# Neighbouring matmuls of one shape, one scan of both heads, and tiles projected a slot ahead in a fused Mamba layer and FFN

## The reference, cut to what matters

```python
proj = einsum('bsd,de->bse', rmsnorm(x), in_proj_w)       # z, x|B|C, dt
xBC = silu(conv4(proj[x|B|C]) + conv_b)                   # 4 taps along the tokens
dA = exp(softplus(dt_raw + dt_bias) * -exp(A_log))
h = dA_t * h + (dt_t * x_t) * B_t                         # for each token, 64x64 per head
y = h . C_t + D * x
g = groupnorm(y * silu(z)) * gate_norm_w
out = residual + g @ out_proj_w
```

## Time and profile before

| what | value |
|---|---|
| median of 3 runs (lowest, highest) | 1144.11 us (1141.79, 1144.46) |
| profiled execution, its span | 1145.73 us, 1143.9 us |
| busy: PE, PEld, DVE | 1033.2 us (90%), 732.0 us (64%), 1059.9 us (93%) |
| busy: ACT, POOL | 970.0 us (85%), 868.6 us (76%) |
| mean granted PE clock | 0.959 |

### The profile page before, as it was taken

The page is one execution under the profiler, slowest core; times in us unless marked ns, Lnnn a source line. Parts: engine busy times, 40 slices in busy tenths (PEclk is TensorE's granted clock), DMA queues, the critical chain, the costliest instruction groups (busy, mean ns, idle before and its releaser), DMA issues.

```text
span 1143.9 us, 26227 instructions
## 1 busy us (share of the span) xinstructions
PE 1033.2 (90%) x8912; PEld 732.0 (64%) x8912; DVE 1059.9 (93%) x2004; ACT 970.0 (85%) x2836; POOL 868.6 (76%) x596
## 2 busy tenths in 40 slices
PE   1724789999999999999999999999999999996797
PEld 1603566676666666676666666766666666664576
DVE  7597999999999999999999999999999999989474
ACT  2767898999999999999999999999999999984464
POOL 7300356888888888888888888888888888885765
PEclk9955899999999999999999999999999999997899
DMA  6320000000000000000000000000000000021001
GB/s 170 117 86 0 10 1 2 1 1 2 1 30 2 2 2 29 2 2 2 29 2 2 2 29 2 2 2 29 2 1 1 21 1 2 1 78 46 1 29 46
DMA packets 28084, 22.58 MB, mean 20 GB/s; under 512 B 11696, under 2 KB 22576, under 8 KB 27824
## 3 DMA queue, kind: packets, MB, share of 16 engines
q1 hardware_dynamic: 25136, 20.90, 5.9%
q10 hardware_dynamic: 2816, 0.02, 0.1%
HBM read 12.78 MB, written 8.13 MB: 18 GB/s over the span
## 4 chain that ended last, share of the span: by engine, by line
PE 77%; DVE 14%; issue 3%; POOL 2%; ACT 2%; DMA 0%; POOLq 0%; DVEq 0%; ACTq 0%
PE bank L1713 10%; PE bank L1695 10%; PE bank L1625 8%; PE bank L1727 8%; PE bank L1641 8%; PE bank L1626 6%; PE bank L1627 6%; PE bank L1681 5%; PE bank L1662 5%; DVE conv L1191 4%; PE bank L1766 3%; PE bank L1738 2%; DVE lm L1181 2%; PE bank L1555 1%; PE bank L1746 1%
## 5 line engine op out<-in xcount | busy, mean ns | idle before, releaser
L1191 DVE SCALAR_TENSOR_TENSOR conv<-bank,cw,conv 128x509 f32<-128x509 f32 (+2 forms) x576 | 421.7, 743 | 16.6 <-ACT conv L762 8.6
L636 POOL TENSOR_TENSOR lm<-lm,cbs 128x1024 f32<-128x1024 f32 x128 | 304.3, 2377 | 75.7 <-ACT xw L866 75.7
L1181 DVE TENSOR_TENSOR_SCAN lm<-bank,ident 128x512 f32<-128x512 f32 x256 | 298.7, 1210 | 0.7 <-PE bank L1641 0.6
L911 ACT ACTIVATE xdt<-bank,dt_all 128x64 f32<-128x64 f32 x1024 | 222.3, 329 | 37.2 <-PE bank L1662 37.2
L866 ACT ACTIVATE xw<-xdt,lm 128x64 f32<-128x64 f32 x768 | 199.3, 365 | 0.0
L644 POOL TENSOR_TENSOR ssum<-ssum,sq 128x512 f32<-128x512 f32 x96 | 123.1, 1283 | 93.0 <-ACT sq L926 92.8
L1625 PE MATMUL bank<-xn_hi,w_hi 128*128 128x512 f32 x320 | 166.1, 519 | 13.8 <-DVE conv L1191 13.1
L615 POOL TENSOR_TENSOR gated<-gated,gate 128x512 f32<-128x512 f32 x128 | 164.9, 1288 | 15.9 <-DVE gated L1238 14.5
L626 POOL TENSOR_TENSOR gated<-gated,rbs 128x512 f32<-128x512 f32 x120 | 153.8, 1282 | 0.0
L877 ACT ACTIVATE conv<-bank,cb_bias,cw 128x512 f32<-128x512 f32 x189 | 142.6, 781 | 11.5 <-PE bank L1627 7.3
L1713 PEld LDWEIGHTS bank<-lm,xdt 128*64 128x64 f32 x2048 | 110.3, 137 | 63.7 <-issue 63.7
(11 more groups left out here) (217 smaller groups left out, 1766.5 us busy)
## 6 DMA issues: line engine op xcount, KB each, us to landing
lm<-in_L_attn_in_proj_w SPq DMA_DIRECT2D x1, 2048.0 KB, 11.7
xn_scratch<-chan SPq DMA_DIRECT2D x4, 512.0 KB, 4.6
r_stage<-residual_scratch SPq DMA_DIRECT2D x8, 256.0 KB, 2.9
xn_stage<-xn_scratch SPq DMA_DIRECT2D x7, 256.0 KB, 3.2
x_scratch<-r_stage SPq DMA_DIRECT2D x7, 256.0 KB, 2.0
gate<-in_L_attn_hidden_states SPq DMA_DIRECT2D x2, 512.0 KB, 4.6
cdec<-in_L_attn_hidden_states SPq DMA_DIRECT2D x2, 512.0 KB, 7.1
w_out<-in_L_attn_out_proj_w SPq DMA_DIRECT2D x8, 128.0 KB, 3.3
```

Of the source, the lines that this page charges most:

```text
L636: gp.tensor_tensor(lm[:, mr, :, :], lm[:, mr, :, :], cbs[:, :, :], ALU.mult).then_inc(m_done, 1)
L911: act.activation(xdt[:, r, at:at + HP], misc_of("xt", n)[:, at:at + HP], ACT.Copy, scale=dt_h).then_inc(xdt_done, 1)
L1181: V.tensor_tensor_scan(lm[:, m % R, a, :], bc_bank[(3 * m + a) % 2][:, :], ident4[:, :], 0.0, ALU.mult, ALU.add).then_inc(scanned, 1)
L1191: V.scalar_tensor_tensor(out=conv[:, ci % 4, shift:S], in0=tile_bank(b, n, t)[:, 0:S - shift], scalar=cw[:, q, t, KW - 1 - shift:KW - shif ...
```

## The change

1. **Side by side.** On PE, `states`, `y_within` and `y_states` of a slot follow each other (`inner`), and the spread rows of the running products and of the next pair's first head come ahead of them; the second head's row comes behind.
2. **One scan.** The two spread rows of the decays lie in two neighbouring banks (`decays`), and DVE scans both heads in one instruction of 1024 columns. The row of the second head now waits for `decay_c` of the pair before it, in the same bank.
3. **State steps.** The copy of the first chunk's state goes from DVE to ACT (`first_state`). The chunks' end products are taken once for all, by 16 small products and one copy in slot 4 of the first sequence; the copy in each slot (L1221) goes.
4. **Second slot a slot early.** Tiles 3 and 4 are projected at the end of the first slot (`next_tile`), around `cb_products`, and ACT begins them there (`next_convolve`); `weigh` of the second slot is also done there (`weigh(1)`). `variance` and its copy go to the end of the first slot.
5. **Order of the second slot.** `b_transposes` comes ahead of `out_product`, `factor_transposes` behind it, z last.
6. **Factors.** The root is taken in POOL's second slot, and POOL instead of ACT copies it to 512 columns (`rexp`).
7. **Out product.** Its operands change places: four products with 128x128 pieces of `gated` as weights and 128 columns of `w_out`, so rows come out token-major; ACT's copy and PE's four transposes at a sequence's end go, and DVE adds the residual from the bank a slot earlier (`output_rows`).

DVE's taps come before `decay_c`, and its state steps behind it, in all slots (not shown). Cut to its core:

```diff
+def early_tile(b, n, t):
+    return n % R == 1 and t in PLAN[1] and (b, n) != (0, 1)
...
             n = 4 * q + r
+            plan += [(n, "xt", LAG_SSD, 0), (n, "s", LAG_STATE, 0)]
             if r == 0:
-                plan.append((n, "var", LAG_VAR, 0))
-            if r < 2:
-                plan += [(n, "s", LAG_STATE, 0), (n, "xt", LAG_SSD, 0)]
-            else:
-                plan += [(n, "xt", LAG_SSD, 0), (n, "s", LAG_STATE, 0)]
-            if r == 0:
-                plan += [(n, "cb", LAG_SSD, 0), (n, "cb", LAG_SSD, 1)]
+                plan += [(n, "cb", LAG_SSD, 0), (n, "cb", LAG_SSD, 1), (n, "var", LAG_VAR, 0)]
             if r == 1:
-                plan.append((n, "bt", LAG_M, 0))
-                plan.append((n, "rbc", LAG_FACTOR, 0))
+                plan += [(n, "bt", LAG_M, 0), (n, "rbc", LAG_FACTOR, 0)]
             if n == XO_SLOT:
-                plan.append((n, "xo", SLOTS, 0))
+                plan.append((n, "unused", SLOTS, 0))
...
+                    after(gp, rstd_done, UNITS, bb, v)
+                    after(gp, rbc_ready, UNITS, bb, v - 1)
+                    gp.tensor_copy(rexp[:, :, :], rtok[:, :].unsqueeze(2).broadcast_to([P, 2 * CH, HP])).then_inc(rexp_done, 1)
...
                 gate_product()
                 if r == 0:
                     decay_product()
                     normalise()
+                elif r == 1:
+                    normalise()
                     root()
+                    decay_product()
+                    square_sum()
...
+                def first_state():
+                    if back(b, n, LAG_STATE) is None:
+                        return
+                    bb, m = back(b, n, LAG_STATE)
+                    after(act, s_ready, SLOTS, bb, m)
+                    after(act, y_ready, SLOTS, bb, m - 2)
+                    act.activation(hpk[:, m % 2, 0, :], misc_of("s", n)[:, 0:NS], ACT.Copy).then_inc(hfirst, 1)
+                def next_convolve(k):
+                    if real and early_tile(b, n + 1, PLAN[1][k]):
+                        begin(PLAN[1][k], n + 1)
...
                     weigh()
                     convolve()
                     activate(0)
+                    scale_x()
+                    first_state()
+                    square()
+                    gate_silu()
+                    weigh(1)
+                    next_convolve(0)
+                    copy_cb()
+                    next_convolve(1)
                     copy_variance()
+                elif r == 1:
+                    convolve()
+                    activate(0)
+                    first_state()
                     scale_x()
                     square()
+                    copy_bt()
+                    copy_factor()
                     gate_silu()
-                    copy_cb()
-                elif r == 1:
...
-                    for a in range(2):
-                        after(dve, bc_ready, 3 * SLOTS, bb, 3 * m + a)
-                        V.tensor_tensor_scan(lm[:, m % R, a, :], bc_bank[(3 * m + a) % 2][:, :], ident4[:, :], 0.0,
-                                             ALU.mult, ALU.add).then_inc(scanned, 1)
+                    after(dve, bc_ready, 3 * SLOTS, bb, 3 * m + 1)
+                    V.tensor_tensor_scan(lm[:, m % R, :, :].rearrange("p a s -> p (a s)"), decays[:, :], ident4[:, :], 0.0,
+                                         ALU.mult, ALU.add).then_inc(scanned, 1)
...
-                    if c == 0:
-                        after(dve, s_ready, SLOTS, bb, m)
-                        after(dve, y_ready, SLOTS, bb, m - 2)
-                        V.tensor_copy(hpk[:, m % 2, 0, :], sbank[:, 0:NS]).then_inc(hstep, 1)
+                    if c == 1:
+                        after(dve, hfirst, SLOTS, bb, m)
+                        if (bb, m) == (0, 0):
+                            dve.wait_ge(pend_done, 1)
                     else:
-                        after(dve, hstep, 3 * SLOTS, bb, 3 * m + c - 1)
-                        V.scalar_tensor_tensor(out=hpk[:, m % 2, c, :], in0=hpk[:, m % 2, c - 1, :],
-                                               scalar=pend[:, m % R, c:c + 1], in1=sbank[:, NS * c:NS * c + NS],
-                                               op0=ALU.mult, op1=ALU.add).then_inc(hstep, 1)
...
-                i = 3 * m + k
-                pm, pk = divmod(i - 2, 3)
-                if pk < 2:
-                    after(pe, scanned, 2 * SLOTS, bb, 2 * pm + pk)
+                if k == 1:
+                    after(pe, cdec_done, SLOTS, bb, m - 1)
                 else:
-                    after(pe, cdec_done, SLOTS, bb, pm)
+                    after(pe, scanned, SLOTS, bb, m - 1 if k == 0 else m)
                 if isinstance(bb, int) and (bb, m, k) == (0, 0, 0):
                     pe.wait_ge(pr_rest, len(PR_ORDER))
                 first = (0, P, HP)[k]
...
+                def next_tile(k):
+                    if real and early_tile(b, n + 1, PLAN[1][k]):
+                        project(b, n + 1, PLAN[1][k], (b, n + 1))
...
-                    last = MM(out_bank[:, :], w_out[:, m, :], gated[:, (m // R) % 2, m % R, :], start=(m == 0), stop=(m == SLOTS - 1))
+                        after(pe, x1_done, 1, bb, -1)
+                        if bb == 0:
+                            pe.wait_ge(pend_done, 1)
+                    for c in range(CH):
+                        tok = slice(P * c, P * c + P)
+                        last = MM(out_bank[:, tok], gated[:, (m // R) % 2, m % R, tok], w_out[:, m, :],
+                                  start=(m == 0 and c == 0), stop=(m == SLOTS - 1 and c == CH - 1))
...
+                def inner():
+                    states()
+                    y_within()
+                    y_states()
                 if r == 0:
                     out_product()
                     tiles()
-                    variance()
-                    states()
+                    transposes()
                     gate_tile()
-                    transposes()
-                    y_within()
                     rows(ssd, 2)
                     rows(ahead, 0)
-                    y_states()
+                    inner()
+                    rows(ahead, 1)
+                    next_tile(0)
                     cb_products()
+                    next_tile(1)
+                    variance()
                 elif r == 1:
                     tiles()
-                    states()
                     transposes()
-                    out_product()
-                    y_within()
                     rows(ssd, 2)
                     rows(ahead, 0)
-                    y_states()
+                    inner()
+                    rows(ahead, 1)
+                    b_transposes()
+                    out_product()
+                    factor_transposes()
                     gate_tile()
-                    b_transposes()
-                    factor_transposes()
                 elif r == 2:
                     tiles()
                     transposes()
-                    states()
+                    rows(ssd, 2)
+                    rows(ahead, 0)
+                    inner()
+                    rows(ahead, 1)
                     out_product()
-                    y_within()
+                    gate_tile()
+                else:
+                    tiles()
+                    transposes()
+                    out_product()
+                    gate_tile()
                     rows(ssd, 2)
-                    y_states()
-                    gate_tile()
                     rows(ahead, 0)
-                else:
-                    transposes()
-                    states()
-                    tiles()
-                    gate_tile()
-                    y_within()
-                    rows(ssd, 2)
-                    out_product()
-                    rows(ahead, 0)
-                    y_states()
+                    inner()
+                    rows(ahead, 1)
                     next_input()
-                    last_output()
-                rows(ahead, 1)
```

200 lines of the change are left out of this document (81 added, 119 removed).

## The result

The changed kernel takes **1179.3 us** (median of 4 runs, 1176.4 to 1180.1) against 1144.3 for the kernel before on the same chip: a ratio of **1.030 [1.027, 1.033]**, slower, and outside the range of 1121 to 1155.

The account below looks back on a forecast made before the run. PE bounded the kernel before; after the change, an ACT-PE loop of 28.48 us a unit. Steady part -3.8, start -1, tail +3 on 1145.7, then 1.6 off to the median: about 1142 us, range 1121 to 1155.

Parts of the forecast that it names:

- PE's work: PE's matmuls in a unit, four units a sequence: cheaper in the new order, 27.0 us needed instead of 28.6.
- DVE's work: DVE's steps in a unit: copies and one scan start leave each slot, about 1.0 us less, 27.3 of 28.3 remain.
- ACT: ACT's list in a unit: loses the root's copy, gains four state copies at 0.20 us each; about even.
- POOL's: POOL's added 512-column copy, one a unit: between nothing and 1.28 us, about 1.0 in the tail; room for it.
- The turn is 28.48 us, longer than any engine's work: Loop of ACT (12.76 + 8.14) and PE (7.58) through `cbs` and `variance`, setting the unit's time; chance 0.45.
- Variance: End of the first slot: PE waits some 1.5 us a unit at `variance` for ACT's copy of `cbs`.
- Start: Before the steady part: DVE saves, slot 4 gains products and a copy; -1 us, bounds -5 and +3.
- Tail: After the last sequences: POOL's root and copy come behind feed-forward additions, PE's factors wait; +3 us, bounds 0 and +7.
- PE does not wait at `variance`: Rival, end of the first slot: a loop through DVE's scans decides, 27.85 us a unit, 1125 us; chance 0.24.
- The state copies lengthen ACT's turn: Rival, ACT's list: state copies at up to 0.33 us each make a unit 28.87, about 1153 us; chance 0.21.
- Bare weight loads: Rival, out product on PE: exposed loads add 0.64 us a slot, 29.5 a unit, about 1168 us; chance 0.04.
- DVE as the bound: Rival: DVE set the pace all along, 27.3 us a unit, 110.4 a sequence, 1110 us; chance 0.06.

Follow-up runs that it names:

- the last version: Changed kernel with variance and next input earlier, three DVE edits, POOL's decay product first, root and out product earlier in the tail: 1140.7 us, 0.997 of the kernel before.

## Why the prediction was wrong, point by point

- **PE's work** (28.6 to 27.0): right in its terms, as far as rows show them (0.40, 0.98, 0.80, an out product 0.81 to 0.90). Busy time could not have shown it: 114.59 us of a sequence against 115.44 in the earlier trace rows; why it hardly fell is not shown. The Trainium skill (Perfetto Trace Analysis, Identifying the Most-Contended Engine) says that matmul busy time is no good measure of headroom; this trace agrees.
- **DVE's work** (28.3 to 27.3): mis-sized. Busy time, 112.28 a sequence less 1.2, in four, is 27.8. Steps from start to start, waits left out, show where it went: a sequence of DVE's list took 114.7 us and now takes 113.0. The copies, the scan and `decay_c` gave back 4.1, as priced (0.25 in each of 16 slots); but the state steps took 1.0 more and the taps 1.3 more. Taps, copies and `decay_c` had stood between steps that wait for each other, and in the first and the fourth slot some of these stand back to back now: two state steps take 0.51 (584.70 to 585.21), where each takes 0.18 beside a tap (577.48 to 577.66); the last section has the taps. In the last version the list takes 113.2 of a sequence's 114.2.
- **ACT** about even: right; a state copy steps 0.10 to 0.15 us, half of what I took. **POOL's** copy was 0.61 (I took about 1.0).
- **"The turn is 28.48 us, longer than any engine's work"**: this is the step that failed, in two ways. It summed ACT's list as if it ran almost without a gap: reckoned 20.90, measured 21.47 (573.15 to 594.62), with gaps of 0.16, 0.4 and POOL's 0.12 in it; PE's part is 7.85 instead of 7.58. And it looked for a loop of two engines, where the round goes through four. What was not priced is what part 5 ties together: `out_product` stands behind the rows, the groups and B, with DVE's `skip` of the same slot waiting on it, and the text never follows who waits for `out_step`. That ties DVE to the end of PE's second slot, PE's second slot to ACT's copy, that copy to POOL's leg and the fourth slot, and the fourth slot to DVE again. The product's place alone is not the cost: put back ahead of the rows it changed nothing, since the row and the states behind it tie the same slot to DVE and ACT, and the fastest version keeps part 5's order in the steady part. What cost time is the length of that round, 29.33 us where DVE's own work is 27.8: 0.9 us less in PE's second slot made a plain unit 0.9 shorter, 0.44 more in ACT's fourth slot made it 0.46 longer. A unit takes 29.5, over the 28.9 that I had named as my bound.
- **Variance**: PE waits there for `cbs`, as said; it is 0.4 us instead of 1.5, and taking the variance off that place gave 14 us. So the place was right and the loop around it was not.
- **Start** (-1, bounds -5 and +3): +2.0 to the first mark, within the bounds.
- **Tail** (+3, bounds 0 and +7): +13.4. The mechanism (root behind the feed-forward step) is right and its size wrong: it held up the second-last unit too, and in the traces 4 to 8 us hang on it. The out product behind the rows, which I had not looked at there either, holds some 2 more; the rest stays open.
- **Rivals**: "PE does not wait at `variance`" did not come true; it waits, and no unit got shorter. "The state copies lengthen ACT's turn" had the direction and named the fourth slot, where ACT "gets there with almost nothing in hand", but not the cause: the copies cost half of what I took, and 0.44 us more in the third slot cost nothing. Bare weight loads: no, 0.81 to 0.90. DVE as the bound: not in the changed kernel, where it waits for 5 us of a sequence; in the kernel before and in the last version it waits for about 1 us and is nearly full (99% and 98% busy), but its work was 27.8 a unit and not 27.3.

## What to carry to other kernels

When a step is moved down an engine's list, follow every semaphore that it raises to whoever waits on it, buffers that it frees included, and at the same slot: a lag of 15 against one of 7 and a ring of 8 made the consumer's write wait for a product in its own slot. A closed round of waits always adds up to the period, so adding one up proves nothing; a known piece of extra work, put into one slot after another, tells which parts decide, and costs one run each. Removing the wait that shows on the busiest engine may only hand it on, if what is late is the block that it waited for. And a small step that is taken out or moved may have been what kept two dependent ones apart.

## What I had not expected of the hardware

A DVE step that reads what the step right ahead of it wrote, and waits for its semaphore, costs some 0.1 us more than the same step with another one between: 0.51 for two state steps of 64 columns against twice 0.18. The taps of 512 columns show it too. Two taps of two different tiles side by side, in the kernel before, and two of the same tile, in the changed kernel, each with the next step:

```profile
534.10 1.38 DVE L1191 SCALAR_TENSOR_TENSOR conv<-bank,cw,conv 128x511 f32<-128x511 f32 x2
535.40 0.21 DVE L1210 COPY hpk<-bank 128x64 f32<-128x64 f32 x1
```

```profile
582.02 1.51 DVE L1197 SCALAR_TENSOR_TENSOR conv<-bank,cw,conv 128x511 f32<-128x511 f32 x2
583.45 0.68 DVE L1229 TENSOR_TENSOR cdec<-decays,chan 128x512 f32<-128x512 f32 x1
```

They take 1.30 and 1.43 us from start to next start. And PE showed 97% busy in a sequence although, by the steps above, some 1.6 us a unit of its work had gone.
